# Edge attribute loads of a graph kernel: issued by ScalarE inside the edge loop instead of by SyncE between mask loads

## The reference, cut to what matters

```
# layer 0
edge_input = concat([x[src], edge_attr_32])            # 96 + 32 features per edge
messages   = gelu(edge_input @ mW1 + mb1) @ mW2 + mb2
gates      = sigmoid(gelu(edge_input @ gW1 + gb1) @ gW2 + gb2)
aggregated = segment_sum(messages * gates, dst)
update     = gelu(concat([x, aggregated]) @ uW1 + ub1) @ uW2 + ub2
x = layernorm(x + layernorm(x + update) * ln_g + ln_b)
# layer 1
Q, K, V = x @ Wq + bq, x @ Wk + bk, x @ Wv + bv        # 8 heads of 12
score = exp(clip(sum(K[src] * Q[dst] * E) / sqrt(12), -5, 5))   # E from edge_attr_96
x = layernorm(x + segment_sum(V[src] * score, dst) / (segment_sum(score, dst) + 1e-6))
```

## Time and profile before

| what | value |
|---|---|
| median of 3 runs | 1260.01 us |
| the profiled execution: its own time / its span | 1260.09 us / 1258.3 us |
| POOL busy | 945.6 us, 75% |
| PE, DVE, ACT busy | 76%, 74%, 55% |
| granted TensorE clock, mean | 0.902 |
| DMA traffic | 178.07 MB, mean 142 GB/s |

### The profile page before, as it was taken

The page is one execution under the profiler, slowest core; times in us unless marked ns, Lnnn a source line. Parts: engine busy times, 40 slices in busy tenths (PEclk is TensorE's granted clock), DMA queues, the critical chain, the costliest instruction groups (busy, mean ns, idle before and its releaser), DMA issues. The chain is left out here.

```text
span 1258.3 us, 18104 instructions
## 1 busy us (share of the span) xinstructions
PE 959.2 (76%) x4628; PEld 580.5 (46%) x4628; DVE 935.4 (74%) x4244; ACT 690.8 (55%) x1522; POOL 945.6 (75%) x984
## 2 busy tenths in 40 slices
PE   5789999989988898888887006887777786787780
PEld 2334444448777677777675003443333333333330
DVE  3435454547999999999999604999777877787873
ACT  2445555533788888888888703555444443444441
POOL 6677777777777777777777777777777777777777
PEclk9889999999999999999998558999888888788875
DMA  5975555444677777777775432333222322222320
GB/s 126 198 194 182 178 183 182 104 140 128 201 219 226 234 224 222 229 235 220 224 230 175 153 78 65 96 88 86 74 74 74 74 74 74 74 75 73 82 59 29
DMA packets 131946, 178.07 MB, mean 142 GB/s; under 512 B 75125, under 2 KB 76852, under 8 KB 131841
## 3 DMA queue, kind: packets, MB, share of 16 engines
q1 hardware_dynamic: 97741, 130.13, 35.5%
q0 software_dynamic: 31360, 46.18, 14.9%
q10 hardware_dynamic: 2740, 0.60, 0.3%
HBM read 101.31 MB, written 77.56 MB: 142 GB/s over the span
## 5 line engine op out<-in xcount | busy, mean ns | idle before, releaser
L399 POOL DMA_INDIRECT out<-wide,put_at x196 | 192.9, 984 | 59.7 <-issue 57.6
L364 POOL DMA_INDIRECT agg_d<-wide,put_at x196 | 191.2, 976 | 61.9 <-issue 55.5
L355 POOL DMA_INDIRECT wide<-in_x,src_i x196 | 185.5, 946 | 69.5 <-issue 58.1
L392 POOL DMA_INDIRECT node_work<-agg_d,src_i x196 | 188.1, 960 | 59.7 <-issue 57.0
L380 POOL DMA_INDIRECT wide<-agg_d,dst_at x196 | 187.7, 957 | 60.1 <-issue 49.7
L635 ACT ACTIVATE node_work<-node_work,nshift,nscale 128x96 f32<-128x96 f32 x392 | 145.7, 454 | 75.7 <-DVE nshift L885 75.6
L673 ACT ACTIVATE nT<-ps 96x512 f32<-96x512 f32 x99 | 57.0, 592 | 169.5 <-PE ps L418 169.4
L418 PE MATMUL ps<-ident,node_work 128*96 128x128 f32 x196 | 32.9, 293 | 133.7 <-DMA node_work<-agg_d,src_i 133.7
L508 PE MATMUL ps<-uW2s,nT 97*128 97x96 f32 x784 | 98.8, 279 | 45.1 <-ACT nT L653 45.1
L767 DVE SCALAR_TENSOR_TENSOR ps<-hidden,ps 96x512 f32<-96x512 f32 x49 | 33.9, 692 | 128.4 <-ACT hidden L616 128.4
L508 PEld LDWEIGHTS ps<-uW2s,nT 97*128 97x128 f32 x784 | 91.6, 192 | 55.1 <-ACT nT L653 55.1
(11 more groups left out here) (156 smaller groups left out, 2267.8 us busy)
## 6 DMA issues: line engine op xcount, KB each, us to landing
agg_d<-zeros SPq DMA_DIRECT2D x40, 480.0 KB, 4.3
x_in<-in_x SPq DMA_DIRECT2D x49, 384.0 KB, 3.2
node_work<-agg_d SPq DMA_DIRECT2D x49, 384.0 KB
agg_d<-node_work SPq DMA_DIRECT2D x49, 384.0 KB, 3.5
out<-node_work SPq DMA_DIRECT2D x49, 384.0 KB
mask<-cont_d SPq DMA_DIRECT2D x49, 208.0 KB
mask<-cont_d SPq DMA_DIRECT2D x49, 192.0 KB, 3.3
ea<-in_edge_attr SPq DMA_DIRECT2D x48, 192.0 KB, 3.7
```

What stands on the lines that cost most here:

```text
L355: pool.indirect_dma_start(rows[:, g * EJ + j, :], None, x, rows_at(src_i, g, j)).then_inc(xs_gathered[g % 2], 16)
L364: pool.indirect_dma_start(agg_d, rows_at(put_at, g, j), rows[:, g * EJ + j, :], None).then_inc(agg_added[g % 2], 16)
L392: pool.indirect_dma_start(ahead[:, g % AHEAD, j, :], None, x1_d, rows_at(src_i, g, j)).then_inc(x1s_gathered[g % 2], 16)
L399: pool.indirect_dma_start(out, rows_at(put_at, g, j), rows[:, g * EJ + j, :], None, bounds_check=N - 1, oob_is_err=False).then_inc(out_sca ...
```

## The change

Loads 0 and 1 stay where they are. Loads 2 to 5 leave SP. Load 2 is issued by ScalarE right before its edge loop; load k for k = 3, 4, 5 at the top of ScalarE's edge step i with i + 10 = EA_FROM[k], which are the steps 6, 17 and 28. The small second part of load 5 moves with it. Sizes, destinations and semaphores stay.

```
+EA_LEAD = 10
...
                 sp.dma_start(wide[:, a:b, D:D + DE], ea32[a * P:b * P, :].rearrange("(j p) f -> p j f", p=P)).then_inc(ea32_loaded[k], 16)
-                if EA_FROM[k + 1] == EGROUPS:
-                    sp.dma_start(wide[0:ETAIL_P, TFULL, D:D + DE], ea32[TFULL * P:E, :]).then_inc(ea32_loaded[k], 16)
...
-                if 2 <= g < len(EA_FROM) - 1:
-                    edge_attributes(g)
...
             act.wait_ge(weights_made, 5)
+            def edge_attributes(k):
+
+                a, b = EA_FROM[k] * EJ, min(EA_FROM[k + 1] * EJ, TFULL)
+                act.dma_start(wide[:, a:b, D:D + DE], ea32[a * P:b * P, :].rearrange("(j p) f -> p j f", p=P)).then_inc(ea32_loaded[k], 16)
+                if EA_FROM[k + 1] == EGROUPS:
+                    act.dma_start(wide[0:ETAIL_P, TFULL, D:D + DE], ea32[TFULL * P:E, :]).then_inc(ea32_loaded[k], 16)
+
+            edge_attributes(2)
+
             def edge_step(i):
                 s = i % 2
+                if i + EA_LEAD in EA_FROM[3:-1]:
+                    edge_attributes(EA_FROM.index(i + EA_LEAD))
```

## The result

The changed kernel takes 1263.78 us (median of 10 runs, 1262.0 to 1266.32), the kernel before 1260.36 us (median of 10 runs in the same comparison). The ratio is 1.0028, with a 95% interval of 1.002 to 1.0037: slower by 3.4 us, 0.28%. That is inside the stated range (1256.3 to 1265.5), but 0.9 us more than the 2.5 us within which I had called it no change, and it is the time of rival B (1263.6). The profiled execution of the changed kernel took 1264.5 us of its own time with a span of 1262.7 us.

What follows compares the result with a forecast made beforehand. POOL's lists of indirect transfers were taken as the bound. From 1260.09 us, -3.46 (today's two waits) + 3.5 (two new ones) + 0 (SP) + 0 (ScalarE) gave 1260.1 us, range 1256.3 to 1265.5.

Steps and rivals of the forecast that it cites:

- rival B: Edge stage: the loads hold POOL more than today, four waits of 1.75 us, giving 1263.6 us; chance 0.23.
- two to three waits: Main forecast: POOL is held by two to three of the four moved loads, time about 1260.1 us; chance 0.53.
- My own sign of being wrong: Start of POOL's scatter list moves by more than 2.5 us, or a later stage moves although that start does not.
- what bounds the kernel: The end is the sum of POOL's five lists of 196 indirect transfers; only POOL's waits change it.
- SP's and ScalarE's terms: Edge stage: SP losing five issues and ScalarE gaining five, with a 7.7 us pause, each change the end by 0.
- C: Rival: masks still wait on SP because descriptor making is shared between queues; end still 1260.1 us; included in the 0.53.
- D: Rival: ScalarE's pause reaches POOL, needing over 27 us; chance 0.02 together with a wholly different cost.
- the remaining term: Edge stage: gathers landing late beside a large load cost POOL 1.75 us per case, bounded at 0 to 7.0 us.
- I take two of four, as in the trace: Edge stage: two of the four moved loads hold POOL, 2 x 1.75 = 3.5 us.
- the net term: POOL's waits in the edge stage: -3.46 us for today's two, +3.5 us for two new ones.
- the place in the load is as good as drawn: Edge stage: for the later two loads, tenths per step decide where a group's last gather falls, so waits were bounded.
- the time of the steps: Forecast issue times on ScalarE: load 2 at 15.1 us, loads 3 to 5 at 51.5, 104.7 and 157.9 us.

Runs made afterwards that it cites:

- e7: Changed kernel with the small second part of load 5 issued at ScalarE's step 24, four steps before the large part; 1265.9 us, ratio 1.0029 to the kernel before.
- e12: Changed kernel, POOL waiting for gathers of four groups earlier instead of two, two setup counters merged; 1717.71 us, ratio 1.0038 to the kernel before in its job.

## Why the prediction was right or wrong

**The number.** The time lies in the range, but not where the sum put it: 1263.78 us against 1260.1. The forecast of two to three waits had a chance of 0.53; what came was rival B, four waits of 1.75 and 1263.6 us, with 0.23. The range holds the time only because it was drawn to take in rival B. My own sign of being wrong, a start of the scatter list more than 2.5 us later, was just met: 255.70 before, 258.25 after.

**Right: what bounds the kernel.** In both profiles POOL's lists fill the time to the end; 2.0 us less of edge stage and 10.0 us less of waiting for masks moved nothing.

**Right: SP's and ScalarE's terms are 0.** Masks go in 0.3 us, C fell. ScalarE pays 0.38 to 0.40 for a large load (0.43 forecast) and 5.76 for the small part (7.3 forecast), and the waits for `einT` stay at 0.3. e7 takes the pause away and changes nothing for the better. D fell. (SP held four times before, not three: the mask behind load 3 took 7.76 us. The sum doesn't use it.)

**Right: the mechanism of the remaining term.** The price of a late group was put at 1.75 us; the four are 1.51 to 1.75. That it came out so close is in part luck: over the sixteen loads of the four kernels it goes from 0.72 to 3.32. That zeros and masks beside a load would draw it out, as rival B also had it, wasn't seen: loads 2 to 4 land 11.8 to 11.9 us after their issue, and a large load before at most 11.8.

**Wrong in size: "I take two of four, as in the trace".** It was four, 6.7 us where the sum had 3.5, so the net term was +3.2 and not 0. The trace before showed two waits for four loads because the loads were 8.7 us apart, so each second one met a GpSimd that had just been held; that sentence stood in the prediction and in rival B, but the sum took the two as a rate. The rows of the kernel before show the two hidden groups. The last gather of group 6 starts at 38.74 us, 0.1 before load 3, and that of group 9 at 55.39, 1.15 before load 5; each time POOL was then held for another group and needed them only 7.9 and 8.0 us later instead of 6.25:

```profile
38.74 0.95 POOL L355 DMA_INDIRECT wide<-in_x,src_i  x1 [0.30 <-issue]
...
46.66 0.94 POOL L355 DMA_INDIRECT wide<-in_x,src_i  x1 [0.30 <-issue]
...
55.39 0.94 POOL L355 DMA_INDIRECT wide<-in_x,src_i  x1 [0.30 <-issue]
...
63.40 0.94 POOL L355 DMA_INDIRECT wide<-in_x,src_i  x1 [0.30 <-issue]
```

The step that failed is "the place in the load is as good as drawn". It took the case of group 7, which cost nothing 6.57 us behind load 3, for a place that a lone load could meet. GpSimd's groups come every 5.0 us, and places from -0.5 to 4.2 us have now been seen to cost. A window of at least 4.7 us, against a beat of 5.0, leaves a load hardly a place to miss. Against B, I had held that the place wasn't known for three of the four. It needn't have been.

**Half right: the time of the steps.** Loads 2 and 4 went at 15.01 and 104.91 us (15.1 and 104.7 forecast), load 3 three us earlier than forecast, load 5 five later. By then the edge steps can't run ahead of the gathers any more: at 114.39 us PE waits 2.65 us for the gather that POOL waits for at 114.60.

**Left open:** the 2.4 us that the profile shows in the scatter list and at its end, and why a gather lands later beside such a load. With the slow jobs, the direct test of the remedy (a wider allowance for GpSimd, expected to bring both kernels to 1257 us) has no result, and no version that beats both kernels was found.

## What to carry to other kernels

Count a wait per event, not per trace: where two of four equal transfers cost something and the others follow closely behind, ask whether the first wait hid the second before taking "two of four" as a rate. Spreading bunched transfers over time can cost more than the bunch, if each of them makes the bounding engine miss a landing deadline that is shorter than the transfer. And to relieve an engine that isn't the bound was worth nothing here, while its transfers remained a load for the engine that is.

## What the runs showed of the hardware

- A group's gathers land within 6.25 us of the start of the last one in the steady state, or POOL would wait for them. Beside a load of 704 KB in rows of 128 bytes they take 7 to 9.6 us (6.25 plus 0.7 to 3.3, by POOL's waits for all sixteen lone loads), whichever of the two queues the load is on.
- Such a load holds its issuing engine for only 0.4 us, but a transfer that follows soon on the same engine's queue is held, for 3.7 to 8 us: until 7.4 to 8.4 us after the load's issue on SP, where zeros and masks stand in the same queue, and until 6.1 and 6.2 us on ScalarE. One that came 11.3 us behind a load was not held (0.31 us). Masks on SP's queue are not held by a load on ScalarE's (at most 477 ns). Here the Trainium skill's "Perfetto Trace Analysis", section "DMA Instruction — HWDGE (DVE, Sync)", describes the descriptor generator as shared by the sequencers and locked for exclusive use until a transfer's descriptors are made. The trace shows nothing of such a lock beyond the 0.4 us: the mask issued at 51.22 us, inside load 3, took 0.30 us, and the one at 165.61, while ScalarE was held at the small part (163.28 to 169.04), took 0.31.

```profile
165.61 0.31 SPq L278 DMA_DIRECT2D mask<-cont_d  x1
```
- A transfer at the top of ScalarE's step went out when the activation ahead of it started, not when it ended: load 3 went at 48.48 us, and the Tanh in front of it ran from 48.47 to 49.15; loads 4 and 5 went at 104.91 and 162.87, with a Tanh from 104.90 and 162.87.
- In five of seven jobs every kernel had a median of 1710 to 1727 us, on four different chips, one of which also gave the usual 1263. GpSimd's transfers were as long as ever there, the other three compute engines stood between instructions again and again (ScalarE in e12 for up to 16.1 us). The mean granted clock was 0.78 in e12 and 0.90 in the kernel before at its usual time; whether that is cause or effect isn't shown. The cause is open.
